# First attention of a two-layer transformer kernel: the order of SyncE's write and read of the relative scores

## The reference

```python
x = L0_attn_x                                  # (32, 256, 128)
xn = _layernorm(x)
x = x + _L0_attn_ref(xn, ...) + _L0_ffn_ref(xn, ...)
xn = _layernorm(x)
x = x + _L1_attn_ref(xn, ...) + _L1_ffn_ref(xn, ...)

# in _L0_attn_ref, with R = 64, s = 256:
dist = jnp.clip(idx[None, :] - idx[:, None], -R, R) + R
pe_k = rel_emb_k[dist]; pe_v = rel_emb_v[dist]
score = einsum('bhqd,bhkd->bhqk', q, k) + einsum('bhqd,qkd->bhqk', q, pe_k)
attn = softmax(score)
ctx = einsum('bhqk,bhkd->bhqd', attn, v) + einsum('bhqk,qkd->bhqd', attn, pe_v)
return ctx @ W_out + b_out
```

## Time and profile before

| | us |
|---|---|
| median of 3 runs (lowest to highest) | 2499.93 (2491.85 to 2500.97) |
| the profiled execution's own time | 2499.09 |
| its span, first to last instruction | 2497.3 |
| busy in the span: PE, DVE, ACT, POOL | 2200.2, 1921.7, 1711.4, 842.6 |
| first and last start of L963, VectorE's copy (256 times) | 435.1, 1543.5 |

### The profile page before, as it was taken

One profiled execution on the slowest core, in us unless ns is written; L12 is line 12 of the kernel. 1 busy time (PEld: TensorE's weight loads), 2 busy tenths in 40 slices (PEclk: granted clock), 3 DMA queues, 4 the chain that ended last, 5 costly groups with the idle time before them and its releaser, 6 DMA issues. The chain is left out here.

```text
span 2497.3 us, 91017 instructions
## 1 busy us (share of the span) xinstructions
PE 2200.2 (88%) x34464; PEld 1779.8 (71%) x34464; DVE 1921.7 (77%) x7669; ACT 1711.4 (69%) x5582; POOL 842.6 (34%) x911
## 2 busy tenths in 40 slices
PE   6999998788888888888888888979999699999998
PEld 5888887577777777777677777657877466666665
DVE  6787772567877777777777777758888598898888
ACT  2333332677777777777677777966666599999998
POOL 3666665020222211122122212321212556566562
PEclk9999999799999999999999999989999799999999
DMA  7867552666676667676666666013231111111110
GB/s 237 238 164 192 115 119 43 160 161 159 170 174 161 167 166 168 168 171 169 166 171 169 168 167 154 23 66 119 95 111 69 47 27 42 30 36 38 27 39 14
DMA packets 360774, 304.80 MB, mean 122 GB/s; under 512 B 25368, under 2 KB 328856, under 8 KB 358952
## 3 DMA queue, kind: packets, MB, share of 16 engines
q1 hardware_dynamic: 349864, 271.93, 43.2%
q0 software_dynamic: 10496, 27.28, 3.7%
HBM read 166.43 MB, written 132.69 MB: 120 GB/s over the span
## 5 line engine op out<-in xcount | busy, mean ns | idle before, releaser
L819 ACT ACTIVATE probs<-neg_scores,low 128x256 f32<-128x256 f32 (+1 forms) x1152 | 574.0, 500 | 227.2 <-DVE low L955 210.6
L955 DVE CUSTOM_DVE_ANT_0 neg_scores<-scores,rel_bias 128x256 f32<-128x256 f32 x1024 | 373.4, 421 | 231.3 <-PE scores L1124 110.2
L1114 PE MATMUL scores<-k_heads,q_heads 32*128 32x256 f32 (+1 forms) x2304 | 208.4, 426 | 162.7 <-DVE rel_s L963 136.3
L1136 PE MATMUL probsT<-consts,probs 128*128 128x128 f32 x2240 | 315.9, 284 | 5.1 <-issue 4.7
L1687 DVE CUSTOM_DVE_ANT_0 neg_scores<-scores,alibi 128x128 f32<-128x128 f32 (+1 forms) x896 | 265.9, 353 | 57.4 <-PE scores L1743 54.0
L771 POOL TENSOR_SCALAR q_heads<-q_raw,consts,q_bias 128x256 f32<-128x256 f32 x128 | 69.4, 557 | 614.2 <-ACT q_raw L802 614.1
L1136 PEld LDWEIGHTS probsT<-consts,probs 128*128 128x128 f32 x2240 | 245.7, 143 | 37.6 <-issue 10.6
L1114 PEld LDWEIGHTS scores<-k_heads,q_heads 32*128 32x128 f32 x2304 | 99.4, 186 | 225.8 <-DVE low L955 154.1
L274 POOL TENSOR_TENSOR hid<-hid,gate_bc 128x512 f32<-128x512 f32 x160 | 205.3, 1288 | 151.6 <-DVE hid L445 144.2
L300 ACT ACTIVATE ga<-gate_up 128x512 f32<-128x512 f32 x160 | 95.6, 598 | 223.3 <-PE gate_up L511 221.6
L963 DVE COPY rel_s<-scores 128x768 f32<-128x768 f32 x256 | 244.0, 953 | 4.2 <-PE scores L1124 2.8
(11 more groups left out here) (204 smaller groups left out, 4983.3 us busy)
## 6 DMA issues: line engine op xcount, KB each, us to landing
rel_rows<-rel_s SPq DMA_DIRECT2D x256, 192.0 KB
rel_bias<-rel_rows SPq DMA_DIRECT2D x256, 192.0 KB, 3.6
gate_bc<-gate_rows SPq DMA_DIRECT2D x32, 1024.0 KB, 10.7
rel_rows<-rel_s SPq DMA_DIRECT2D x256, 128.0 KB
rel_bias<-rel_rows SPq DMA_DIRECT2D x256, 128.0 KB, 3.6
packed<-ffn_in SPq DMA_DIRECT2D x8, 1280.0 KB, 15.7
xe<-packed SPq DMA_DIRECT2D x16, 640.0 KB, 3.9
expert_out<-ye POOLq DMA_DIRECT2D x16, 640.0 KB, 3.2
```

The lines of the kernel that those rows point to most:

```text
L819: act.activation(probs[s % 3][:, j, 0:w], neg[s % 2][:, j, 0:w], ACT.Exp, bias=low[s % 3][:, j:j + 1], scale=-1.0, accum_out=sums[s // UB ...
L955: dve.tensor_tensor_reduce(neg[s % 2][:, j, 0:w], S_ps[:, 512 * j:512 * j + w], bias_of(s)[:, j, :] if s < NU0 else alibi[:, 4 * j + s % 4 ...
L1114: ins = pe.matmul(S_ps[:, 512 * j:512 * j + w], q_of[b % 2][rows, i, qt * P:(qt + 1) * P], k_of[b % 2][rows, 0:w], start=True, stop=True)
L1136: ins = pe.transpose(PT_ps[kt][:, j * P:(j + 1) * P], probs[u % 3][:, j, kt * P:(kt + 1) * P], ident)
```

## The change

The loop of SyncE's queue no longer reads unit u - 1 behind the write of unit u, but unit u behind its own write. The read of the last unit, which stood behind the loop, falls away, since the loop now holds it. The helper functions, with their waits, are as they were. The order of issues was w0 w1 r0 w2 r1 w3 r2 ..., and is now w0 r0 w1 r1 w2 r2 ...

```diff
                 for u in range(NU0):
                     write_relative(u)
-                    if u >= 1:
-                        read_bias(u - 1)
+                    read_bias(u)
                     b, r = divmod(u, UB)
                     if r == 6:
                         load_norms(b + 2)
                     if r == 2 and b >= 5 and b % 2 == 1:
                         store_xn2T((b - 5) // 2)
-                read_bias(NU0 - 1)
                 load_norms(nb + 2)
```

## The result

The changed kernel takes 2847.4 us (median of four runs, 2843.1 to 2849.5) against 2498.0 us before: a ratio of 1.140, 95% interval 1.138 to 1.141. The direction and the mechanism of the forecast came true. The size did not: the time lies 172 us above the forecast and 47 us above the range.

What follows compares the result with a forecast made beforehand. It took waits between TensorE and VectorE, 4.35 us per unit, as the bound; SyncE's 3.5 + 1.37 + 0.04 + 0.14 = 5.05 us would replace it, adding 179.4 us, less 2.2: forecast 2675 us, range 2555 to 2800.

Steps and rivals of the forecast that it cites:

- The bound now: First attention, 434 to 1560 us: no engine is full; waits between TensorE and VectorE set 4.35 us per unit.
- (a): Bias reads issued some 2.1 us earlier, so most of VectorE's 70.9 us of bias waits would go.
- The ring of TensorE and VectorE: The two engines hand score banks to and fro in the first attention, 4.35 us per unit.
- (b): SyncE's queue waits every unit for the write's landing: 3.5 us from first issue to release, bounds 3.23 and 4.5.
- (c): Rest of SyncE's unit: read issues 1.37 us, gap to next write 0.04, loads and stores 0.14.
- (d): First attention: SyncE becomes the bound at 5.05 us per unit, never short of input; write(0) to write(255) grows 179.4 us.
- The Trainium skill's figure: DMA landing by the skill's formula: 4.55 us per unit, total near 2548 us; the prediction went by the trace instead.
- R1: Rival, faster: write lands within SyncE's idle time, 2.9 us or less after first issue; 2430 to 2450 us; 6 in 100.
- R2: Rival, worse: writes queue behind reads in the DMA queues; 6.1 us per unit, 2940 us; 12 in 100.
- R3: Rival: TensorE's clock falls as it is less busy; if low with projections too, 3020 us; 3 in 100.
- The signs named beforehand: Expected profile: L709 wait almost nothing, L720 near 580 us, bias wait 250 or more, L963 span 1285, DMA share 0.59.

## Why the prediction was wrong in size

*The bound now* and *(a)*: right. The ring of TensorE and VectorE at 4.35 us was the one to beat, and 70.9 us all there was to gain. Even with the read out as early as possible and nothing queued behind it, 61.6 us of it stayed.

*(b), the wait for the landing*: the mechanism was right in place, in who stands behind it and in every unit, and its size failed. The step said "I take 3.34 + 0.15 = 3.5 us, near the measured writes, because the reads ahead have had 1.3 us to drain". Measured: 4.19 us. Its two parts: in an empty queue without a fetch 3.34 us, as put; the reads ahead without a fetch 3.47 to 3.34, so 0.13 us, as put (0.15). What was missing is the instruction fetch: 145 of 256 writes have one start in their first 3.0 us and land 1.0 us later than the others, which is 0.55 of the 0.69 us. Both writes that the step rested on stood at the ends of the stage, where the profile of before shows no packet of q8 in either write's time, and an average cannot be read from two samples. That the 3.34 us agree so well with units that meet nothing is part luck: they are the mean of 3.23 and 3.45. The row that held the information stood in the term of the range: the xn2T store in midstream at 3.9 us, and, on the page, q8's 268 packets. I gave the first as the upper bound, 0.6 + 3.9 = 4.5 us, and then chose the value nearest to the samples taken out of the crowd. The measured mean lies 0.3 us under that bound.

*(c), the rest of SyncE's unit*: 1.37 + 0.04 + 0.14 = 1.55 us was put, 1.29 + 0.22 = 1.51 us measured. The long read issues of the earlier trace rows are nearly gone: both issues took about 1.26 us in nine tenths of the units, and over 1.8 us in 4 units, against 63 before. The write's took 1.23 us on average instead of 1.21.

*(d), the stage*: 255 x 5.05 was put and 255 x 5.70 is what came; the difference of 0.65 us is 166 of the 172 us by which the forecast is short. That SyncE never starves held (19.7 us in all, 10.8 of it the first). Not foreseen was that VectorE's copy waits 97.8 us for the write of two units earlier. It stands in the shadow of the same period.

*The Trainium skill's figure* (2.0 us plus bytes / 436e3, in "DMA: Bandwidth & Descriptors", section "Anatomy of one DMA", fitted on GpSimd's path) would have given the estimate of 2548 us; the measured landing time, 4.19 us, is further from it than the two samples were. The outcome agrees with the rule of the same page of the Trainium skill, section "Rules for kernel authors", to issue a transfer early and wait late: the wait that came at once cost 340 us.

*The rivals*: R1 fell, since even the shortest landing time was 3.23 us. R2 (writes queue behind reads, 6.1 us per unit, 2940 us) was nearest in number, mostly by luck: queueing behind the reads has a price of 0.13 us, where R2 had over 1 us, and the fetches gave the rest. The 5.70 us lie inside R2's 5.5 to 6.1, to which I gave 12 in 100: too low. R3's first half came true, TensorE's granted clock fell to 0.89, and decided nothing: SyncE's sum accounts for the period, and with one write and one read SyncE's sum and the period fell together, to 4.86 us.

*The signs named beforehand*: L709's wait went to almost nothing, VectorE's bias wait over 250 us, its wait for TensorE's scores shrank (99.6 to 22.3 us), the spans before the stage and after the last copy stayed (953.8 and 957.5 us). One had the wrong direction: TensorE's wait for VectorE's copy was to shrink and rose from 124.9 to 345.2 us, since the copy comes later in a period that SyncE sets. L720's wait was put at 580 us and is 736; L963's distance at 1285 and is 1448; the DMA share at 0.59 and is 0.49. The first two misses are the same 0.65 us per unit. For the third it gives only 0.52 (0.68 x 4.35 / 5.70); the transfers also took less time of the engines.

Open: how a fetch holds up a write. Where it starts explains part of the spread (above), and a fetch without the crowd costs as much as one within it, 1.0 us in 13 writes. But copies in packets of the same 16 KB cost 0.28 us at most, so a held engine alone is not shown to be the cause.

## What to carry to other kernels

In an in-order issuing queue, put nothing that another engine needs behind a wait for a landing; here the wait was free in a queue where nothing urgent stood behind it (720 us of it cost nothing) and cost 340 us with the next write behind it. For a period that one queue sets, take the landing time from transfers in the thick of the stage, and look in the DMA queues for instruction fetches that fall on it (here 1.0 us for 145 writes of 256); the two samples at this stage's ends met none. And before moving a wait, try fewer, larger DMAs in the old order: one write for two brought 1.1% here, where the reordering cost 14%. Last, when a control is to show that packets are large or small, count them by size: their number alone, 32 a copy in both layouts, hid two packets of 16 KB.

## What the runs showed of the hardware

- An instruction fetch of 16 KB takes a DMA engine about 1.13 us (127 packets, 0.9% of 16 engines over 1000 us). A write of 320 KB with one starting in its first 3.0 us lands 1.0 us later (4.62 against 3.64 us); one that starts 1.5 to 3.0 us into the write costs 1.0 us in empty engines too (4.42 against 3.38, 13 writes), and one that starts up to 1 us before the write next to nothing (3.40 against 3.36). Leaving out about a third of TensorE's instructions of a unit took 49 us off a stage in which TensorE was not the bound.
- A copy within HBM as two rows of 16 KB went as 2 packets of 16 KB from either queue, with 2 packets of 4 bytes beside them from SyncE and 30 from GpSimd. Sixteen rows of 2 KB went as 16 packets of 2 KB and 16 of 4 bytes from both.
- At the same number of bytes the two large packets cost a write 0.28 us more than the sixteen small ones (3.60 against 3.32 us), when SyncE issued them just ahead of it.
- GpSimd issues a 192 KB or 128 KB copy of 256 rows in 0.63 us, SyncE in 0.61 (medians of 512).
